# Weight loads in order of need, three query groups ahead of N, FFN weight scaling in slices, and the LoRA matmuls in column groups

## The reference

```python
h = layernorm(x)                                   # no affine
q, k, v = h @ Wq.T + bq, h @ Wk.T + bk, h @ Wv.T + bv
s = abs(q @ k.T) / 32                              # scores * their sign, causal
out = softmax(causal(s)) @ v @ Wo.T + bo
x = x + layernorm(out)
w = round(kernel / scale) clipped to int4, * scale # scale = max|kernel| / 7
y = layernorm(x) @ w + bias + (layernorm(x) @ a) @ b   # a: 1024x16, b: 16x1024
x = x + layernorm(y)
```

## Time and profile before

| | us |
|---|---|
| median of 3 runs (one of them at 2144.89) | 1840.89 |
| lowest | 1840.31 |
| the profiled execution | 1837.48 |
| its span, core 5, first to last instruction (all cores 1832.1 to 1835.9) | 1835.9 |

### The profile page before, as it was taken

How to read it: one execution, slowest core, us unless ns; L and a number is a source line. 1 busy time by engine, 2 the same in 40 slices (tenths; PEclk the granted TensorE clock), 3 DMA queues, 4 the chain that set the end, 5 groups by cost and what they waited for, 6 DMA issues and landing times.

```text
span 1835.9 us, 27208 instructions; the slowest of 8 cores (1832.1 to 1835.9 us)
## 1 busy us (share of the span) xinstructions
PE 1742.5 (95%) x8491; PEld 785.9 (43%) x8491; DVE 957.3 (52%) x1751; ACT 656.0 (36%) x841; POOL 329.0 (18%) x958
## 2 busy tenths in 40 slices
PE   3698889999999999999999999999999999999996
PEld 1243334444444444444444444444444444444442
DVE  2525665555532355555445556666566656543433
ACT  3232323333322334433334433434343343433431
POOL 1332111111100011111111122222222222111111
PEclk9899999999999999999999999999999999999998
DMA  9868789866631334544454465697445454434231
GB/s 303 227 198 218 178 201 208 217 173 155 150 101 52 66 95 102 153 118 107 114 164 96 96 168 131 179 258 194 123 119 133 126 124 125 112 84 99 57 86 46
DMA packets 355872, 259.50 MB, mean 141 GB/s; under 512 B 280449, under 2 KB 313601, under 8 KB 351634
## 3 DMA queue, kind: packets, MB, share of 16 engines
q1 hardware_dynamic: 304514, 164.95, 39.4%
q10 hardware_dynamic: 51216, 92.81, 15.6%
HBM read 122.44 MB, written 67.11 MB: 103 GB/s over the span
## 4 chain that ended last, share of the span: by engine, by line
PE 88%; DVE 3%; issue 3%; DMA 2%; POOL 2%; ACTq 1%; ACT 1%; SPq 0%; DVEq 0%; POOLq 0%
PE O L400 25%; PE S L381 24%; PE F L422 11%; PE S L315 11%; PE F L348 6%; PE O L348 5%; PE F L426 2%; PE X L412 2%; DMA wst<-wq 1%; PE F L334 1%; PE O L334 1%; ACTq L793 1%; ACTq L612 1%; DVE fq L519 0%; DMA xr<-x 0%
## 5 line engine op out<-in xcount | busy, mean ns | idle before, releaser
L381 PE MATMUL S<-hT,Gq 128*128 128x512 bf16 (+3 forms) x2304 | 466.8, 361 | 1.1 <-ACT SA L719 1.1
L400 PE MATMUL O<-V,PT 128*128 128x512 bf16 x2112 | 467.0, 379 | 0.0
L381 PEld LDWEIGHTS S<-hT,Gq 128*128 128x128 bf16 x2304 | 221.3, 98 | 246.5 <-issue 1.6
L719 ACT ACTIVATE SA<-S,cq 128x512 f32<-128x512 f32 (+3 forms) x288 | 185.4, 651 | 390.4 <-PE S L381 382.3
L400 PEld LDWEIGHTS O<-V,PT 128*128 128x128 bf16 x2112 | 201.5, 98 | 260.8 <-issue 26.3
L315 PE MATMUL S<-hT,M 128*128 128x512 bf16 x1024 | 237.6, 386 | 23.8 <-ACT Gst L687 22.7
L422 PE MATMUL F<-W,h2T 128*128 128x512 bf16 x1024 | 235.8, 384 | 8.8 <-DVE xr L604 8.8
L561 DVE TENSOR_REDUCE st<-SA 128x1 f32<-128x512 f32 (+3 forms) x288 | 175.0, 634 | 70.6 <-ACT SA L719 63.7
L672 ACT ACTIVATE h<-xr,stA 128x1024 bf16<-128x1024 f32 x60 | 74.4, 1240 | 284.6 <-DVE junk L494 230.8
L315 PEld LDWEIGHTS S<-hT,M 128*128 128x128 bf16 x1024 | 100.9, 99 | 149.7 <-issue 34.3
L728 ACT ACTIVATE P<-SA,st 128x1280 bf16<-128x1280 f32 (+13 forms) x104 | 142.3, 1369 | 52.0 <-DVE st L570 50.5
(11 more groups left out here) (114 smaller groups left out, 1242.4 us busy)
## 6 DMA issues: line engine op xcount, KB each, us to landing
xr<-x SPq DMA_DIRECT2D x128, 512.0 KB, 4.8
y<-xr ACTq DMA_DIRECT2D x64, 512.0 KB, 2.7
g_scr<-Gst ACTq DMA_DIRECT2D x64, 256.0 KB, 3.6
Gq<-g_scr SPq DMA_DIRECT2D x64, 256.0 KB, 3.0
h_scr<-hT SPq DMA_DIRECT2D x8, 1024.0 KB, 8.4
v_scr<-V ACTq DMA_DIRECT2D x8, 1024.0 KB, 8.4
hT<-h_scr ACTq DMA_DIRECT2D x8, 1024.0 KB, 7.7
V<-v_scr ACTq DMA_DIRECT2D x8, 1024.0 KB, 10.8
```

The source lines that it names most:

```text
L381: mm = t.matmul(out=SR[(j + 2) % 3][:, 0:wd], lhsT=Gq[:, (i % 3) * 1024 + dc * 128:(i % 3) * 1024 + (dc + 1) * 128], rhs=hT[:, sl * 4096 + ...
L400: mm = t.matmul(out=O[:, hh * 512:(hh + 1) * 512], lhsT=PT[:, (i % 2) * 4096 + blk * 128:(i % 2) * 4096 + (blk + 1) * 128], rhs=V[:, sl * ...
L719: s.activation(out=SA[:, c * 512:c * 512 + wd], in_=SR[(j + 2) % 3][:, 0:wd], func=AF.Abs, bias=cq[:, seq * 32 + tile:seq * 32 + tile + 1] ...
```

## The change

- **Loads.** All loads of the start are on SP's queue: row blocks of Wq and the low halves of Wk in turns, seven constants, the high halves of Wk, x tiles 0 to 3; then Wv and WoT blocks as steps `WL` between the groups. ACT casts the two halves of Wk apart (`cast_hi`). The second half of M runs with k outside and c inside. gc comes before u.
- **Steps.** `T` is split: `T` transpose, `X` load of x, `L` statistics and scale, `H` normalise, `J` the dot with u, `HS` store of h_scr, `C` POOL cast of a weight block. G(0), G(1), G(2) come before bo and N; V 0 to 11 follow N; from a = 3 on the order of G and V is as before. `wvb` lies over `wqb`, so the Wv casts wait for u.
- **FFN weights.** The kernel slices are loaded at V 0 to 7, one maximum is taken per V step, and one slice is quantized per step (`Z`) over eight steps; `ZB` scales b and bias.
- **LoRA.** `a_bf` has 32 columns for each of the eight blocks, and the eight matmuls go to four column groups of 32 (tile_position (0, q)), so that X0 holds four partial sums. `xaT` and `B4` have 128 rows: b four times, bias in row 16, zero elsewhere; VectorE adds `one16` while it copies.
- **Order of phase B.** The small tiles of `BORD` are spread differently.

```diff
-    out = [("T", n) for n in range(4)]
...
+    out = [("WL", 0), ("WL", 1), ("C", 0, 1), ("C", 1, 1)]
+    for n in range(4):
+        out += [("T", n), ("X", n + 4), ("L", n + 4)]
+    out += [("C", 0, 0), ("C", 1, 0), ("WL", 2), ("WL", 3), ("C", 2, 1), ("C", 2, 0), ("C", 3, 1), ("C", 3, 0)]
     for c in range(8):
         out.append(("G", 0, c))
+        if c < 4:
+            out += [("H", 4 + c), ("T", 4 + c), ("X", 8 + c), ("J", 4 + c)]
+    out += [("WL", 4), ("WL", 5)] + [("L", n) for n in range(8, 12)]
+    out += [("C", 4, 1), ("C", 4, 0), ("C", 5, 1), ("C", 5, 0)]
+    for c in range(8):
+        out.append(("G", 1, c))
+        if c < 4:
+            out += [("H", 8 + c), ("T", 8 + c), ("X", 12 + c), ("J", 8 + c)]
+    out += [("WL", 6), ("WL", 7)] + [("L", n) for n in range(12, 16)]
+    out += [("C", 6, 1), ("C", 6, 0), ("C", 7, 1), ("C", 7, 0)]
+    for c in range(8):
+        out.append(("G", 2, c))
+        if c >= 4:
+            out += [("H", 8 + c), ("T", 8 + c), ("X", 12 + c), ("J", 8 + c), ("J", c - 4)]
+    out.append(("bo",))
+    for c in range(8):
+        out.append(("N", c))
         if c % 2:
-            out.append(("T", 4 + c // 2))
-    out += [("G", 1, c) for c in range(8)]
-    out.append(("bo",))
-    out += [("N", c) for c in range(8)]
-    for k in range(8):
-        if k < 6:
-            out.append(("T", 8 + k))
+            out.append(("L", 16 + c // 2))
+    for k in range(12):
+        if k in (0, 2):
+            out += [("H", 16 + k // 2), ("T", 16 + k // 2), ("X", 20 + k // 2), ("L", 20 + k // 2), ("J", 16 + k // 2)]
+        elif k in (4, 6, 8):
+            out.append(("H", 16 + k // 2))
+        if k in (5, 7, 9, 11):
+            out.append(("HS", k // 2 - 2))
         out.append(("V", k))
-    out.append(("fkmax",))
-    for a in range(2, 16):
+        if k >= 4:
+            out.append(("fkmax", 11 - k))
+    for a in range(3, 16):
         for k in range(4):
             if a == 3 and k in (0, 2):
                 out.append(("Q", k // 2))
-            if 4 * a + 6 + k < NA:
-                out.append(("T", 4 * a + 6 + k))
+            n = 4 * a + 6 + k
+            if n < NA:
+                out.append(("T", n))
+            if n + 4 < NA:
+                out += [("X", n + 4), ("L", n + 4)]
+            if n + 3 < NA:
+                out.append(("H", n + 3))
+            if n < NA:
+                out.append(("J", n))
+            if n % 4 == 1 and 4 <= n // 4 - 1 < 8:
+                out.append(("HS", n // 4 - 1))
             out += [("G", a, 2 * k), ("G", a, 2 * k + 1), ("V", 4 * a + k)]
+            if (a, k) == (3, 2):
+                out.append(("ZB",))
+            z = 4 * a + k - 14
+            if 0 <= z < 8:
+                out.append(("Z", 7 - z))
...
-BORD = [(0, t) for t in (19, 31, 10, 30, 4, 29, 5, 28, 6, 27, 7, 26, 8, 25, 9, 24, 11, 23, 12, 22, 13, 21, 14, 20, 0, 18, 1, 17,
-                         2, 16, 3, 15)]
-BORD += [(1, t) for t in (11, 10, 9, 8, 15, 14, 13, 12, 16, 0, 17, 1, 18, 2, 19, 3, 20, 4, 21, 5, 22, 6, 23, 7, 24, 25, 26, 27,
-                          28, 29, 30, 31)]
...
+BORD = [(0, t) for t in (19, 31, 10, 30, 0, 29, 11, 28, 1, 27, 12, 26, 2, 25, 13, 24, 3, 23, 14, 22, 4, 21, 9, 20, 5, 18, 8, 17,
+                         6, 16, 7, 15)]
+BORD += [(1, t) for t in (11, 10, 9, 8, 15, 14, 13, 12, 16, 17, 0, 18, 19, 1, 20, 21, 2, 22, 23, 3, 24, 25, 4, 26, 27, 5, 28, 29,
+                          6, 30, 7, 31)]
...
-        with nc.sbuf_tensor("wqb", [128, 8192], BF16) as wqb, nc.sbuf_tensor("wkb", [128, 8192], BF16) as wkb, \
-                nc.sbuf_tensor("wvb", [128, 8192], BF16) as wvb:
+        with nc.sbuf_tensor("wqb", [128, 8192], BF16) as wqb, nc.sbuf_tensor("wkb", [128, 8192], BF16) as wkb:
...
-            for c in range(8):
-                t.wait_ge(m_evv if c % 2 else m_eva, c // 2 + 1)
-                for k in range(8):
+            for k in range(8):
+                t.wait_ge(casth_d, k + 1)
+                for c in range(8):
+                    if k == 0:
+                        t.wait_ge(m_evv if c % 2 else m_eva, c // 2 + 1)
                     mm = t.matmul(out=MB[c], lhsT=wqb[:, k * 1024 + c * 128:k * 1024 + (c + 1) * 128],
                                   rhs=wkb[:, k * 1024 + 512:k * 1024 + 1024], start=(k == 0), stop=(k == 7))
-                mm.then_inc(m_d, 1)
-            pair_free(t, 0)
+                    if k == 7:
+                        mm.then_inc(m_d, 1)
             t.wait_ge(bias_d, 4)
...
+            t.wait_ge(m_eva, 5)
...
-                mm = t.matmul(out=X0[0:16, 0:128], lhsT=a_bf[:, dc * 16:(dc + 1) * 16],
-                              rhs=h2T[:, o + dc * 128:o + (dc + 1) * 128], start=(dc == 0), stop=(dc == 7))
+                q = 32 * (dc % 4)
+                mm = t.matmul(out=X0[q:q + 32, 0:128], lhsT=a_bf[:, dc * 32:(dc + 1) * 32],
+                              rhs=h2T[:, o + dc * 128:o + (dc + 1) * 128], start=(dc < 4), stop=(dc >= 4),
+                              tile_position=(0, q))
...
+                t.wait_ge(fw_d, 8)
+                t.wait_ge(fb4_d, 1)
...
-                mm = t.matmul(out=F[:, hh * 512:(hh + 1) * 512], lhsT=xaT[0:17, (i % 2) * 128:(i % 2 + 1) * 128],
-                              rhs=B17[0:17, hh * 512:(hh + 1) * 512], start=False, stop=True)
+                mm = t.matmul(out=F[:, hh * 512:(hh + 1) * 512], lhsT=xaT[:, (i % 2) * 128:(i % 2 + 1) * 128],
+                              rhs=B4[:, hh * 512:(hh + 1) * 512], start=False, stop=True)
...
-                if k < 2:
-                    stats(v, 2 * k)
-                    stats(v, 2 * k + 1)
...
             m_evac_v(v, 0)
+            v.wait_ge(cst_ld, 16 * 7)
...
+            for n in range(4):
+                stats(v, n)
             m_evac_v(v, 1)
+            v.wait_ge(gc_d, 1)
+            v.tensor_scalar_mul(out=g0[:], in0=S0[:, 0:9], scalar1=1.0 / 32.0).then_inc(gc_ev, 1)
             v.wait_ge(u_d, 1)
...
-                for s in range(8):
-                    v.wait_ge(w_ld[s], 48)
...
-                v.tensor_scalar(out=wst[:, s * 1024:(s + 1) * 1024], in0=wst[:, s * 1024:(s + 1) * 1024],
-                                scalar1=fq[:, 16:17], scalar2=MAGIC, op0=ALU.mult, op1=ALU.add).then_inc(fw_d, 1)
-            for s in range(8):
-                v.wait_ge(fw_d, s + 1)
...
+            elif kind == "ZB":
+                v.wait_ge(fb_ld, 80)
+                v.tensor_scalar_mul(out=B4[:], in0=fbst[:], scalar1=fq[:, 16:17]).then_inc(fb4_d, 1)
+            elif kind == "Z":
+                v.tensor_scalar(out=wst[:, a * 1024:(a + 1) * 1024], in0=wst[:, a * 1024:(a + 1) * 1024],
+                                scalar1=fq[:, 16:17], scalar2=MAGIC, op0=ALU.mult, op1=ALU.add).then_inc(fz_d, 1)
+                v.wait_ge(fz_d, 9 - a)
+                v.tensor_scalar(out=W[:, a * 1024:(a + 1) * 1024], in0=wst[:, a * 1024:(a + 1) * 1024],
...
+            v.tensor_scalar_add(out=xaT[:, (i % 2) * 128:(i % 2 + 1) * 128], in0=X0[:, 0:128],
+                                scalar1=one16[:]).then_inc(xa_ev, 1)
...
+                s.activation(out=wkb[:, k * 1024:k * 1024 + 512], in_=wst[:, (2 * k + 1) * 1024:(2 * k + 1) * 1024 + 512],
                              func=AF.Identity, scale=1.0).then_inc(castk_d, 1)
-                if k:
-                    merge_load(s, k - 1)
-            merge_load(s, 7)
+            cast_hi(s, 0)
+            cast_hi(s, 1)
             m_evac_s(s, 0)
+            for k in range(2, 8):
+                cast_hi(s, k)
+            for n in range(4):
+                ln1(s, n)
             m_evac_s(s, 1)
...
+            if kind == "H":
+                ln1(s, a)
...
+            for k in range(8):
+                sp.dma_start(out=wst[:, 2 * k * 1024:(2 * k + 1) * 1024],
+                             in_=w_h["wq"][k * 128:(k + 1) * 128, :]).then_inc(w_ld[2 * k], 16)
+                sp.dma_start(out=wst[:, (2 * k + 1) * 1024:(2 * k + 1) * 1024 + 512],
+                             in_=w_h["wk"][k * 128:(k + 1) * 128, 0:512]).then_inc(wl_ld[k], 16)
...
+            for k in range(8):
+                sp.dma_start(out=wst[:, (2 * k + 1) * 1024 + 512:(2 * k + 2) * 1024],
+                             in_=w_h["wk"][k * 128:(k + 1) * 128, 512:1024]).then_inc(w_ld[2 * k + 1], 16)
+            for n in range(4):
+                xa_load(sp, n)
...
+        def merge_load(sp, k):
+            sp.wait_ge(castq_d, k + 1)
+            sp.dma_start(out=wst[:, 2 * k * 1024:(2 * k + 1) * 1024],
+                         in_=w_h["wv"][k * 128:(k + 1) * 128, :]).then_inc(w_ld[2 * k], 16)
+            sp.wait_ge(castk_d, k + 1)
+            sp.wait_ge(casth_d, k + 1)
+            sp.dma_start(out=wst[:, (2 * k + 1) * 1024:(2 * k + 2) * 1024],
+                         in_=w_h["woT"][k * 128:(k + 1) * 128, :]).then_inc(w_ld[2 * k + 1], 16)
...
-                if n == 8:
-                    sp.wait_ge(n_d, 8)
                 if n == 16:
```

(43 more changed lines are left out.)

154 lines of the change are left out of this document (54 added, 100 removed).

## The result

The median of the four executions is 1834.5 us against 1950.9 us for the kernel before in the same session. In two of the four executions of each kernel some cores show a lower granted clock and the time is 80 to 300 us longer, and the comparison leaves these out: the ratio is 0.9748, interval 0.9706 to 0.979. The profiled execution took 1794.5 us. The forecast was 1772 us, -3.7%; the change brought about -2.5%.

A forecast was written before the change was run, and what follows sets the result against it. It took phase A to lose 79.5 us, to late transfers and VectorE blocks, and phase B to be TensorE throughout with F waits and FFN seams. 17 + 17.5 + 12 + 13 + 11 less 1.5 gives 69: 1772 us, range 1755 to 1788.

The forecast's parts named there:

- 4a: FFN seams before and behind line 426: due to the short operand, 128 rows remove 0.11 + 0.10 us per tile, -13 us.
- 4b: Line 412's eight LoRA matmuls in column groups: 0.27 us taken, between 0.2 and 0.66, -11 us.
- new xaT waits: Phase B: a shorter line 412 uncovers waits of 0.2 us at some seven tiles, costing 1.5 us.
- Part 4: FFN of each tile in phase B: line 426's seams go, -13 us, and line 412 gets shorter, -11 us.
- part 3: Phase B, tiny tiles spread apart: TensorE's waits for VectorE to free F go, 12 of the 12.4 us.
- part 1: Phase A up to V(0), loads in order of need: 41 us lost there against 58, -17 us.
- bo to 118.5, N to 146, V(0) at 147: Phase A after G(2), which ends at 115: bo, then N, then the first V group at 147 us.
- the starts of the G groups: Phase A, bound by transfers: G(0) near 55.5 instead of 75.2, G(1) at 77, G(2) at 99.5 us.
- part 2: V stage, VectorE's work no longer in blocks: 4 of the 21.6 us lost there remain, -17.5 us.
- Quantizing is cut into steps: V stage: 8 steps of two 0.67 us passes fit, VectorE being busy 4.8 of 6.9 us per slot.
- The transfers bind more: Rival, chance 0.20: one strictly ordered queue delays G(1), G(2) and V; first two parts give 10, not 34.5 us: 1796.5.
- the other three: FFN gains nothing, 1796 (0.13); line 412's loads don't overlap, 1797 (0.05); column groups run one after another, 1911 us (0.04).

The follow-up runs named there:

- e0: The changed kernel measured again, nothing altered, as reference for the other runs; ratio 0.9741, core median 1787.7 us.
- e5: The changed kernel with the old order of query tiles; core median 1794.2 us, +6.5, ratio 0.9762.
- e7: e6 with the LoRA and bias matmuls reading 17 rows again instead of 128; core median 1816.7 us, +13.7 over e6.
- e6: The changed kernel with the eight LoRA matmuls in one column group instead of four; core median 1803.0 us, +15.2.
- e1: The changed kernel with J steps 0 to 3 at G(2)'s first four chunks instead of its last four; core median 1779.8 us, -8.0.
- e9: e4 with only 256 of 1024 columns of each Wv and WoT block loaded, so another output; core median 1764.0 us, -7.6 against e4.
- e2: The changed kernel with the statistics of tiles 20 and 21 moved behind V(1) and V(3); core median 1778.7 us, -9.1.
- e4: The changed kernel with the edits of e1, e2 and e3 together; core median 1771.6 us, -16.2, ratio 0.9745.
- e3: The changed kernel with normalise, transpose and load steps of tiles 4 to 11 one G chunk earlier; core median 1785.9 us, -1.9.
- e8: e4 with VectorE copying xaT ahead of the row maxima also at four score chunks; core median 1767.1 us, -4.5 against e4.

## Why the prediction was right and wrong

The terms against the runs, on core medians and the medians of the starts (in brackets with the starts of e0, the same kernel):

| term | forecast | measured | from |
|---|---|---|---|
| 1 loads in order of need, up to V(0) | -17 | -2.7 (-6.7) | lost before V(0): 57.2 to 160.0 - 105.5 = 54.5 |
| 2 no blocks in the V stage | -17.5 | -8.2 (-8.9) | V(0) to phase B beyond its matmuls: 435.7 - 414.7 to 413.7 - 400.9 |
| 3 tiny tiles apart | -12 | -6.5 | e5 |
| 4a line 426's seams | -13 | -13.7 | e7 - e6 |
| 4b column groups in line 412 | -11 | -15.2 | e6 |
| new xaT waits | +1.5 | inside 3 and 4b | |
| sum | -69 | -46.3 (-51.0) | core median: -46.2 |

That the sum meets the core median within 0.1 us is luck: the starts of another execution shift it by 5, and phase B gained 32 to 34 us as a whole, not the 35.4 of its three terms.

**Right.** Part 4, the seams. They were read from the earlier trace rows and priced by the difference of two rows of the same kind, and e7 gives them within 2 us (13.7 by the core median, 11.5 by the length of phase B). The sign of line 412 was right too, the size and the reason were not. The sum took 0.35 us to line 422; 0.23 were measured, so the gain per tile was 0.31 us and not 0.17. It let the eight follow one another at the pace of the one-column matmuls, 0.025 us; the single records of the changed kernel show that they run side by side. Four start 0.003 us apart, the other four 0.057 us later, and the eight starts lie within 0.076 us, against 0.401 in e6 (medians over the 64 tiles of core 7). The rule of the Trainium skill, TensorE: Matmul & The Clock Gate, Part 3, that a weight load overlaps only when the row group differs, does not describe this: all loads of line 461 share their rows. The VectorE add on 128 partitions takes 0.35 us where the copy of 16 took 0.28, and not the same.

The forecast also said that phase B would last 1215 us; it lasts 1215.8. This is partly luck, since line 412 gave 4 to 6 us more and part 3 about 5 less than their terms.

**Wrong, part 1: the step from bo to V(0).** "bo to 118.5, N to 146, V(0) at 147" adds TensorE's time alone. It leaves out VectorE: the J(c - 4) steps that the change itself puts into G(2) were overlooked, and with them eight dots, 13.6 us, in one piece ahead of the evacuation of F. This was 5.2 us of wait, on all eight cores, and 5.46 - 3.62 = 1.8 at a lower clock behind it; e1 gives 8.0 us back. From N(0) to V(0) 28.5 us were forecast and 36.3 passed.

**Nearly right, part 1: the starts of the G groups.** On core 7 G(0) came 3.6 us later than forecast, G(1) 7.1, G(2) 9.1, but this is the slowest core. The medians of that execution are 2.8, 4.8 and 4.3 us late, those of e0 0.8, 1.2 and 0.6. So at most some 4 or 5 us of what is missing lie here, and they are no larger than the spread between two executions of the same kernel. The sum takes the transfers as the only thing in the way. e9 (fewer bytes: 7 us at G(2), little before) bears this out for G(2); for G(1) it stays open.

**Wrong, part 2: "Quantizing is cut into steps" costed the blocks, not what was put in their place.** The blocks went, and the two stalls of the earlier trace rows with them. But the statistics of tiles 20 and 21, which in the kernel before came behind V(7), now stand before the evacuations of V(0) and V(2) and wait for a tile whose load is queued behind a transpose: 5.3 us, then 6.03 - 3.61 = 2.4 at the lower clock. e2 gives 9.1 back. From V(0) to phase B 404 us were forecast and 413.7 passed. The 2.9 us for fq were overlooked in the same way; they are still there in e4. With both faults (J and L) mended and e3's step (e4), V(0) is at 150.4 and the V stage loses 406.3 - 400.9 = 5.4 us; 4 were forecast. The forecast for phase A would have been 5 to 6 us from right, had these two steps been checked.

**Mis-sized, part 3.** The waits for F went as forecast (11.3 to 0.6 us). The step "12 of the 12.4 us with them" took it that no other wait appears. (Two tiles at distance 2 have at least 12 blocks together in the new order, 10 and 0, and not 15; these are 5.2 us, still more than the 4.3 needed.) A shorter line 412 and the new order leave 6.9 us at xaT, where it was 3.6 and 1.5 were in the sum; e8 shows the cause, the evacuation behind row maxima, by taking 5.2 of 7.2 us away and 4.5 off the end (5.6 by the length of phase B).

**The rivals.** "The transfers bind more" gave 1796.5, which is near the time, but its mechanism is only part of it: of the 16 us that e4 brings back at most e3's 2 have to do with transfers, while e9 shows another 7.6 us that do. None of the other three happened. No rival named the cause that mattered most, an evacuation queued behind a moved step. The prediction asked for each changed wait what is queued behind it on SP, and not the same of VectorE.
